# One wide fp32 product in place of eight transposes and eight narrow products in the merge stage of a test-time-memory attention and MoE kernel

## The chip, the cores and the metric

The kernel runs on one core of a Trainium2 chip, as one program. The metric is device time in microseconds (us) of the whole program. Three runs of the kernel before the change gave 2380.78, 2381.34 and 2384.04 us; their median is 2381.34 us. The engines are named PE (TensorE), DVE (VectorE), ACT (ScalarE), POOL (GpSimd) and SP (SyncE, which here only issues DMAs). PEld is the weight load of a PE instruction.

## What is computed

Two layers follow each other over x of 8 x 1024 tokens with 256 features: a sliding-window attention with a memory MLP that takes one gradient step (its output is merged with the attention's by two sigmoid gates), and a top-2 mixture of eight experts with a capacity of 640 tokens each. The part that the change touches is the seam between them:

```python
g1 = jax.nn.sigmoid(out_swa @ lin1.T)
g2 = jax.nn.sigmoid(out_mem @ lin2.T)
out_merged = g1 * out_swa + g2 * out_mem
...
x = x + attention_layer(layernorm(x), ...)        # x1, the residual sum
...
h = layernorm(x)                                   # input of the experts
logits = h @ gate_w.T + gate_b                     # 8 columns per token
probs = softmax(logits); topk_prob, topk_idx = top_k(probs, 2)
# the position of each token in its expert's queue is a running count over all tokens
x = x + experts(h, topk_idx, topk_prob)
```

Since the layer norm is (x1 - mean) * rstd, the kernel takes the logits from x1 itself: it multiplies x1 with the gate weights less their mean over the features ("centred gate"), which removes the mean's share, and scales by rstd afterwards.

## The kernel before

Four phases run one after the other: attention, gradient, merge and experts. Products of fp32 accuracy are made of three products of rounded halves (fp32r, `matmul_split`, L105: low x high, high x low, high x high). The change lies in `merge_phase`, which takes the 8192 tokens in 16 chunks (C = 0 to 15) of four blocks of 128 tokens. In it everything of a chunk lies transposed, features on partitions (`ga` is 128 x 2 x 512: two halves of 128 features, 512 tokens), while layer norm, router and output want tokens on partitions.

Each engine has its own list of work, written out by hand; semaphores (`signal`, `wait_ge`) tie the lists together, and a wait holds up everything behind it on its engine. Of one chunk C the PE list has, in this order:

- `hidden(C, 0..7)`: eight tiles of the memory MLP's hidden layer, six products of 512 columns each; behind the second of them `gate2(C-1)`, two tiles of the second gate of the chunk before;
- `residual(C-1, 0)`: eight transposes (L2019) of the merged sum `ga` of chunk C-1 into the PSUM tile `ps_r`, which wait for the sum (`merged`, DVE L2275);
- `router(C-1, 0)`: eight fp32 products (L2038) of the same blocks of `ga` with the centred gate, 8 columns each, two for each block of tokens, which add up in PSUM (`ps_l`, in the tile `ps_s`);
- `gate1(C)`: twelve products;
- `dispatch(C-2)` (from C = 2 on): five bf16 products (L2049, L2051) of the one-hot choices of chunk C-2, which count tokens per expert into `ps_c`, in the tile `ps_s` too; they wait for the one-hots (`chosen`, DVE L2394);
- `memory_out(C, ...)`: the output layer of the MLP, 48 products. In C = 15 a second `dispatch(14)` stands before its last quarter.

The DVE list of a chunk has, in this order: the multiplications of the hidden tiles (L2244), the gates of chunk C-1 and its merged sum (L2275), `weigh(C-2)` (L2372 to L2377), `choose_experts(C-2)` (L2384 to L2394), the rest of hidden tile 7 (`rest_hidden`, L2249), then `norm_stats(C-1)` (L2321 to L2330), DVE's `dispatch(C-2)`, `router(C-1)` (L2353, which scales the logits), `shift`, `norm_apply` and the rests for the next chunk. ACT makes the sigmoids (L2098), rounds the hidden tiles (L2103) and copies the transposed sum from PSUM to SBUF (`copy_x1`, L2159), from where it is stored and normed. POOL makes the rests of hidden tiles 0 to 6 (L2504).

The last chunk's sum (C = 15) is handled behind the loop in two parts.

Of the kernel before, what the change touches and what calls it, by code (L numbers as in the profile page):

```python
# [12 lines left out]
AX = mybir.AxisListType  # L13
# [1798 lines left out]
        sems.give_back(made)  # L1812


def merge_banks():

    out = []
    for C in range(NCH):
        out += [("gate2", C - 1, m) for m in range(KC) if C]
        out += [("gate1", C, m) for m in range(KC)] + [("om", C, m) for m in range(KC)]  # L1820
    return out + [("gate2", NCH - 1, m) for m in range(KC)]


def merge_phase(nc, io, sems, shared, routed, halves, g1, g2, b1n, b2n, chunk_in, first_w1, first_w2):
    with ExitStack() as ctx:
        made = []

        def sb(name, shape, dt=F32):
            return ctx.enter_context(nc.sbuf_tensor(name, shape, dt))
# [30 lines left out]
        x1 = [sb("x1_0", [P, GRP, D]), shared.oT[:].rearrange("p (j d) -> p j d", j=GRP)]  # L1860
        rows = routed.rows
        x2 = sb("xn2_full", [P, GRP, D])
        gate_c, ones_f = sb("gate_centred", [P, KC, E]), sb("m_ones_f", [P, P])
        stats, mv, rstd = sb("m_stats", [P, GRP, 6]), sb("m_mv", [P, GRP, 2]), sb("m_rstd", [P, 2, GRP])
        lg, below, pr = sb("logits", [P, GRP, E]), sb("logits_below", [P, GRP, E + TOPK]), sb("router_probs", [P, GRP, E + TOPK])
        sm = sb("router_sum", [P, 2, GRP])
# [10 lines left out]

        ps_z = [ps(f"m_ps_z{i}", [P, T]) for i in range(NZ)]
        ps_o = [ps(f"m_ps_o{i}", [P, T]) for i in range(2)]
        ps_r = ps("m_ps_r", [P, GRP, D])  # L1880
        ps_s = ps("m_ps_s", [P, 512])
        ps_l, ps_c = ps_s[:, 0:GRP * E], ps_s[:, GRP * E:]
        x1_v = io["out"].rearrange("(b p) d -> p b d", p=P)

        use = merge_banks()
# [14 lines left out]

        z_done = signal("m_z_done", hidden_of)
        gate1_done, gate2_done, om_done = (signal(f"m_{k}_done", kinds[k]) for k in ("gate1", "gate2", "om"))
        merged_T, logits_done = (signal(n, tails) for n in ("merged_T", "logits_done"))
        gate_summed = signal("gate_summed", [0])
        counts_done = signal("counts_done", chunks)

# [52 lines left out]
        def tensor(e):  # L1959
# [52 lines left out]
            def residual(C, n):  # L2012
# [6 lines left out]
                        i = e.transpose(ps_r[:, j, m * P:(m + 1) * P], ga[:, m, j * P:(j + 1) * P], ident[:])  # L2019
                i.then_inc(*merged_T(C, n))  # L2020

            def sum_gate():
                pe.wait_ge(*gate_in.at(0))
                pe.wait_ge(*const_set.at(4))
                for k in range(KC):
                    i = e.matmul(ps_l[:, 0:E], ones_f[:], gate[:, k], start=k == 0, stop=k == KC - 1)
                i.then_inc(*gate_summed(0))
# [13 lines left out]
            def dispatch(C):  # L2041
                pe.wait_ge(*chosen.at(C, 2))
                pe.wait_ge(*earlier_made.at(0))
                pe.wait_ge(*const_set.at(5))
                pe.wait_ge(*lg_scaled.at(C))
                n = SIZES[C]
                out = ps_c[:, 0:(n + 1) * n_hot].rearrange("p (j x) -> p j x", x=n_hot)
                ones_of = hot[:].rearrange("p j k x -> p j (k x)")
                e.matmul(out, earlier[:], ones_of[:, 0:n + 1], start=True, stop=False)  # L2049
                for i in range(n):  # L2050
                    x = e.matmul(out[:, i + 1:], ones[:], ones_of[:, i:i + 1].broadcast_to([P, n - i, n_hot]), start=False, stop=i == n - 1)  # L2051
                x.then_inc(*counts_done(C))

            for C in chunks:
                tail, sent = C >= 1, C >= 2
                hidden(C, 0)
                hidden(C, 1)
                if tail:
                    gate2(C - 1)
                for t in range(2, HC):  # L2060
                    hidden(C, t)
                if tail:
                    residual(C - 1, 0)
                    router(C - 1, 0)
                gate1(C)
                if C == 0:
                    sum_gate()
                if sent:
                    dispatch(C - 2)
                memory_out(C, 0, 0)  # L2070
                memory_out(C, 0, 1)
                memory_out(C, 1, 0)
                if C == NCH - 1:
                    dispatch(NCH - 2)
                memory_out(C, 1, 1)
# [16 lines left out]
        def scalar(e):  # L2092
# [58 lines left out]
            def copy_x1(C, n):  # L2151
# [4 lines left out]
                    act.wait_ge(*x2_made.at(*final_part(C - 2)))  # L2156
                else:
                    act.wait_ge(*x2_made.at(C, n))
                e.activation(x1[s][:, blocks], ps_r[:, blocks], ACTF.Copy).then_inc(*x1_made(C, n))  # L2159

            def split_x2(C, n):
                blocks = parts_of(C)[n]
# [73 lines left out]
        def vector(e):  # L2236
# [95 lines left out]
            def norm_apply(C, n):  # L2332
# [9 lines left out]
                dve.wait_ge(*const_set.at(3))  # L2342
                e.tensor_copy(routed.tails(C)[:, blocks, 0], tokens[:, C * GRP + blocks.start:C * GRP + blocks.stop]).then_inc(*numbered(C, n))

            def router(C):
                n, wide = SIZES[C], [P, SIZES[C], E]
                src = ps_l.rearrange("p (j x) -> p j x", x=E)
                dve.wait_ge(*logits_done.at(*final_part(C)))
                dve.wait_ge(*gate_b_in.at(0))
                dve.wait_ge(*chosen.at(C - 1, 0))  # L2350
                dve.wait_ge(*shifted.at(C - 1, 0))
                dve.wait_ge(*rstd_made.at(*final_part(C)))
                e.tensor_tensor(lg[:, 0:n], src[:, 0:n], rstd[:, 1, 0:n].unsqueeze(2).broadcast_to(wide), ALU.mult).then_inc(*lg_scaled(C))  # L2353
                dve.wait_ge(*lg_scaled.at(C))
# [72 lines left out]
            for C in chunks:  # L2427
# [26 lines left out]
                if C == 0:  # L2454
# [2 lines left out]
                    e.tensor_copy(earlier[:], before_f[:]).then_inc(*earlier_made(0))  # L2457
                    centre_gate()
                if tail:
                    norm_stats(C - 1, 0)  # L2460
                if sent:
                    dispatch(C - 2)
# [76 lines left out]
        def sync(e):  # L2539
# [15 lines left out]
            load_oT(0)  # L2555
            load_x(0)
            e.dma_start(gate[:], io["gateT"].rearrange("(c p) n -> p c n", p=P)).then_inc(*gate_in(0))
            e.dma_start(gate_b[:], io["gate_b"]).then_inc(*gate_b_in(0))
            e.dma_start(ident[:], io["ident"]).then_inc(*ident_in(0))
            e.dma_start(before_f[:], io["before"]).then_inc(*before_in(0))  # L2560
# [494 lines left out]
```

## Time and profile before

| | |
|---|---|
| median of three runs | 2381.34 us |
| the profiled execution's own time | 2381.39 us |
| its span, as the profile shows it | 2379.6 us |
| PE busy | 2335.8 us (98%) |
| DVE busy | 1691.1 us (71%) |
| ACT busy | 1608.7 us (68%) |
| POOL busy | 1394.9 us (59%) |
| the merge loop, chunks 0 to 15 | about 1392 to 1878 us of the span |

The profile is of one execution. The busy time of an engine is the time in which at least one of its instructions ran; matmuls overlap each other in it, so that the distance from start to start of neighbouring matmuls, and not the length of one, tells what one costs. "Idle before" is time in which an engine stood still ahead of an instruction, with what released it; such a releaser is inferred from semaphore events, and "issue" means that the profile shows none.

### The profile page before, as it was taken

Reading aid. Unit: us, or ns where it says so; the run is one execution under the profiler, and the core shown is the slowest. Engines: PE = TensorE matmul, PEld = TensorE weight load, DVE = VectorE, ACT = ScalarE, POOL = GpSimd, SP = SyncE. Lnnn points to the kernel's source line nnn. Section 1 sums busy time; section 2 is a strip of 40 time slices with the busy share of each in tenths; the row PEclk is TensorE's granted clock in tenths of the full one; section 3 lists DMA queues with packets and bytes.
Section 4 is the critical chain, followed back from the end, with each engine's and each line's share of the span. In section 5 each row is a group of like instructions: output and inputs, shape, how many; then the busy total and the mean of one; then the engine's idle time right before and its main releaser. Section 6 shows DMA issues by size and latency. Waiting matters only on the chain. (4 is left out here: it accounts for less than half of the span.)

```text
span 2379.6 us, 40041 instructions
## 1 busy us (share of the span) xinstructions
PE 2335.8 (98%) x14851; PEld 2080.9 (87%) x14851; DVE 1691.1 (71%) x3668; ACT 1608.7 (68%) x2459; POOL 1394.9 (59%) x1000
## 2 busy tenths in 40 slices
PE   7999999999999999999999999999999899999998
PEld 6888888788888888888888978888888789999998
DVE  7777776666666666666666677777777667777776
ACT  5887888757777777777777647777777545554453
POOL 3665566567766766666677735666666543343433
PEclk9999999999999999999999999999999999999999
DMA  4222221542332223222333222333222055555551
GB/s 132 85 84 72 94 76 54 215 126 65 72 69 63 63 64 66 63 62 65 69 68 68 80 92 89 107 103 101 96 91 72 22 156 140 141 151 144 145 141 58
DMA packets 295394, 221.74 MB, mean 93 GB/s; under 512 B 189282, under 2 KB 262023, under 8 KB 295072
## 3 DMA queue, kind: packets, MB, share of 16 engines
q1 hardware_dynamic: 281376, 188.74, 29.1%
q0 software_dynamic: 13824, 30.44, 4.2%
q8 instruction: 118, 1.93, 0.3%
q14 instruction: 76, 0.62, 0.1%
HBM read 113.30 MB, written 72.12 MB: 78 GB/s over the span
## 5 line engine op out<-in xcount | busy, mean ns | idle before, releaser
L2780 ACT ACTIVATE e_hf<-e_ps_z,e_b 128x640 f32<-128x640 f32 x128 | 102.0, 797 | 213.2 <-PE e_ps_z L105 181.3
L2504 POOL TENSOR_TENSOR m_hl<-m_hf,m_hh 128x512 fp32r<-128x512 f32 x112 | 159.6, 1447 | 100.8 <-ACT m_hh L2103 98.5
L2908 POOL DMA_INDIRECT out<-e_ys,slot_token x80 | 83.4, 1042 | 216.3 <-DVE e_ys L2859 210.8
L105 PE MATMUL e_ps_y<-r_w_h,e_hl 128*128 128x256 f32 x640 | 180.3, 282 | 0.1
L105 PE MATMUL e_ps_y<-r_w_l,e_hh 128*128 128x256 f32 x640 | 178.9, 279 | 0.0
L105 PE MATMUL e_ps_y<-r_w_h,e_hh 128*128 128x256 f32 x640 | 178.6, 279 | 0.0
L1686 POOL TENSOR_TENSOR halves_l<-hT_full,halves_h 128x512 fp32r<-128x512 f32 x120 | 153.7, 1303 | 38.2 <-ACT halves_h L1337 38.2
L932 POOL DMA_INDIRECT xbuf_d<-xn,scatter_rows x128 | 139.0, 1086 | 62.3 <-issue 35.6
L789 POOL TENSOR_TENSOR prob<-prob,softmax_small 128x1024 f32<-128x1024 f32 x65 | 123.2, 1896 | 71.1 <-DVE softmax_small L705 71.1
L105 PE MATMUL e_ps_z<-slotsT_h,w_l 128*128 128x320 f32 x512 | 158.9, 310 | 0.7 <-issue 0.7
L105 PE MATMUL e_ps_z<-slotsT_h,w_h 128*128 128x320 f32 x512 | 158.9, 310 | 0.0
L105 PE MATMUL e_ps_z<-slotsT_l,w_h 128*128 128x320 f32 x512 | 158.9, 310 | 0.0
L2244 DVE SCALAR_TENSOR_TENSOR m_hf<-m_ps_z,new_b,m_sig 128x512 f32<-128x512 f32 x128 | 95.9, 749 | 86.1 <-ACT m_sig L2098 63.3
L1544 DVE TENSOR_TENSOR new_w2T<-g_bank,new_w2T 128x512 f32<-128x512 f32 x128 | 88.6, 692 | 92.5 <-PE g_bank L105 92.5
L1331 ACT ACTIVATE hT_full<-h_wordsT 128x2048 uint16<-128x2048 uint16 x60 | 153.2, 2553 | 0.0
L105 PE MATMUL g_bank<-dpred_h,h_l 128*128 128x256 f32 x520 | 147.4, 283 | 1.7 <-DVE shared_x L1537 1.7
L105 PE MATMUL g_bank<-halves_h,keys_l 128*128 128x256 f32 (+1 forms) x528 | 147.4, 279 | 1.1 <-DVE halves_l L1495 1.1
L1551 DVE TENSOR_TENSOR new_w1T<-g_bank,new_w1T 128x512 f32<-128x512 f32 x128 | 88.5, 692 | 83.6 <-PE g_bank L105 83.6
L105 PE MATMUL g_bank<-halves_l,keys_h 128*128 128x256 f32 (+1 forms) x528 | 147.8, 280 | 0.0
L105 PE MATMUL g_bank<-halves_h,keys_h 128*128 128x256 f32 (+1 forms) x528 | 147.3, 279 | 0.0
L105 PE MATMUL g_bank<-dpred_l,h_h 128*128 128x256 f32 x520 | 147.1, 283 | 0.0
L105 PE MATMUL g_bank<-dpred_h,h_h 128*128 128x256 f32 x520 | 147.1, 283 | 0.0
(371 smaller groups left out, 8967.4 us busy)
## 6 DMA issues: line engine op xcount, KB each, us to landing
shared_xT<-xT_d SPq DMA_DIRECT2D x64, 256.0 KB, 3.6
new_w1T<-in_W SPq DMA_DIRECT2D x16, 1024.0 KB
new_w2T<-in_W SPq DMA_DIRECT2D x16, 1024.0 KB
xbuf_d<-new_w1T SPq DMA_DIRECT2D x16, 650.0 KB, 8.4
shared_x<-in_x SPq DMA_DIRECT2D x16, 512.0 KB, 4.1
xn_d<-xn SPq DMA_DIRECT2D x32, 256.0 KB, 2.5
xT_d<-shared_xT SPq DMA_DIRECT2D x32, 256.0 KB, 2.7
oT_d<-shared_oT SPq DMA_DIRECT2D x32, 256.0 KB, 2.6
```

Of the source, the lines that this page charges most:

```text
L105: i = e.matmul(out, a, b, start=first and not onto and n == 0, stop=last and n == len(terms) - 1, skip_group_check=onto)
L789: e.tensor_tensor(p[:], p[:], sm[:, 3].unsqueeze(2).broadcast_to([P, HEADS, 2 * P]), ALU.mult).then_inc(*prob_made(g))
L932: e.indirect_dma_start(io["xbuf_d"][k], bass.IndirectOffsetOnAxis(ap=self.slot[C % 2][:, k, j:j + 1], axis=0), self.rows[C % 3][:, j], Non ...
L1331: e.activation(hT_f[b][:].bitcast(U16).rearrange("p (n s) -> p s n", s=2), wordsT[b][:].rearrange("p (s k) t -> p s (k t)", s=2), ACTF.Cop ...
L1544: e.tensor_tensor(dst, bank("g2", p, t)[:], dst, ALU.add).then_inc(*g2_added(p, t))
L1551: e.tensor_tensor(dst, bank("g1", p, t)[:], dst, ALU.add).then_inc(*g1_added(p, t))
L1686: e.tensor_tensor(hTl[:, ks, block[b]], hT_f[b][:, hc].rearrange("p (k t) -> p k t", k=4), hTh[:, ks, block[b]], ALU.subtract).then_inc(*m ...
L2244: e.scalar_tensor_tensor(hf[r][:, 0:N], ps_z[r][:, 0:N], b1n[:, t:t + 1], sig[r][:, 0:N], ALU.add, ALU.mult).then_inc(*h_made(C, t))
L2504: e.tensor_tensor(hl[:, t, 0:N], hf[(HC * C + t) % NZ][:, 0:N], hh[:, t, 0:N], ALU.subtract).then_inc(*h_low(C, t))
L2780: e.activation(hf[(HC * i + t) % NHF][:].rearrange("p (s n) -> p s n", s=2), ps_z[t % 2][:, :, 0:HALF], ACTF.Relu, bias=b1[:, i % E, t:t + ...
L2908: e.indirect_dma_start(io["out"], bass.IndirectOffsetOnAxis(ap=token[i % 2][:, b:b + 1], axis=0), ys[:, b], None, bounds_check=NT - 1, oob ...
```

## The change

For chunks 0 to 14, `residual` and `router` on PE become one function, `residual_router(C)`. A block of 128 features x 128 tokens of `ga` is loaded as weights once and multiplied, in fp32, with 136 columns: the identity (128) and the centred gate of that half of the features (8). The first 128 columns of the result are the transposed block; the last 8 are this half's share of the logits. The two halves go to different places in PSUM, since the identity columns must not add up; so the shares are summed afterwards, by a new DVE instruction (`sum_logits`), which reads 128 x 4 x 8 x 2 values from PSUM and writes 128 x 32 to `lg` in SBUF. It stands ahead of `norm_stats(C-1)` in the DVE list. L2353 reads `lg` instead of PSUM.

The tiles `ps_r` (two banks) and `ps_s` (one) become one tile `ps_t` of three banks: eight units of 171 columns, three to a bank, so that no product crosses a bank; behind them `ps_l` and `ps_c`. The third bank then holds the units 6 and 7 and the counts of `dispatch`. So PE's `dispatch(C-2)`, in iteration C, gets two waits more: for ACT's copy of the units of chunk C-1 (`x1_made`) and for DVE's sum (`lg_summed`) of chunk C-1. The second dispatch of iteration 15 waits for the same two as its first. The right operand `turned` (identity and gate side by side) gets its identity by two more DMAs of 64 KB, which SP issues at the start of the merge phase ahead of six others. Chunk 15 keeps the old functions, on the new tile.

```diff
--- before.py
+++ after.py
@@ -1812,6 +1812,9 @@
         sems.give_back(made)
 
 
+UNIT = 171
+
+
 def merge_banks():
 
     out = []
@@ -1860,7 +1863,8 @@
         x1 = [sb("x1_0", [P, GRP, D]), shared.oT[:].rearrange("p (j d) -> p j d", j=GRP)]
         rows = routed.rows
         x2 = sb("xn2_full", [P, GRP, D])
-        gate_c, ones_f = sb("gate_centred", [P, KC, E]), sb("m_ones_f", [P, P])
+        turned = sb("ident_and_gate", [P, KC, P + E])
+        gate_c, ones_f = turned[:, :, P:], sb("m_ones_f", [P, P])
         stats, mv, rstd = sb("m_stats", [P, GRP, 6]), sb("m_mv", [P, GRP, 2]), sb("m_rstd", [P, 2, GRP])
         lg, below, pr = sb("logits", [P, GRP, E]), sb("logits_below", [P, GRP, E + TOPK]), sb("router_probs", [P, GRP, E + TOPK])
         sm = sb("router_sum", [P, 2, GRP])
@@ -1877,9 +1881,10 @@
 
         ps_z = [ps(f"m_ps_z{i}", [P, T]) for i in range(NZ)]
         ps_o = [ps(f"m_ps_o{i}", [P, T]) for i in range(2)]
-        ps_r = ps("m_ps_r", [P, GRP, D])
-        ps_s = ps("m_ps_s", [P, 512])
-        ps_l, ps_c = ps_s[:, 0:GRP * E], ps_s[:, GRP * E:]
+        ps_t = ps("m_ps_t", [P, 3 * 512])
+        units = ps_t[:, 0:GRP * KC * UNIT].rearrange("p (j k x) -> p j k x", k=KC, x=UNIT)
+        ps_r = ps_t[:, 0:GRP * D].rearrange("p (j d) -> p j d", j=GRP)
+        ps_l, ps_c = ps_t[:, GRP * KC * UNIT:GRP * KC * UNIT + GRP * E], ps_t[:, GRP * KC * UNIT + GRP * E:]
         x1_v = io["out"].rearrange("(b p) d -> p b d", p=P)
 
         use = merge_banks()
@@ -1900,7 +1905,10 @@
 
         z_done = signal("m_z_done", hidden_of)
         gate1_done, gate2_done, om_done = (signal(f"m_{k}_done", kinds[k]) for k in ("gate1", "gate2", "om"))
-        merged_T, logits_done = (signal(n, tails) for n in ("merged_T", "logits_done"))
+        merged_T = signal("merged_T", tails)
+        logits_done = signal("logits_done", [u for u in tails if u[0] == NCH - 1])
+        turned_in = signal("m_turned_in", range(KC), 16)
+        lg_summed = signal("m_lg_summed", chunks[:-1])
         gate_summed = signal("gate_summed", [0])
         counts_done = signal("counts_done", chunks)
 
@@ -2019,6 +2027,21 @@
                         i = e.transpose(ps_r[:, j, m * P:(m + 1) * P], ga[:, m, j * P:(j + 1) * P], ident[:])
                 i.then_inc(*merged_T(C, n))
 
+            def residual_router(C):
+                pe.wait_ge(*merged.at(C, 0))
+                for k in range(KC):
+                    pe.wait_ge(*turned_in.at(k))
+                pe.wait_ge(*gate_centred.at(0))
+                pe.wait_ge(*x1_made.at(*final_part(C - 1)))
+                if C:
+                    pe.wait_ge(*lg_summed.at(C - 1))
+                if C >= 2:
+                    pe.wait_ge(*placed.at(C - 2, 1))
+                for j in range(SIZES[C]):
+                    for k in range(KC):
+                        i = e.matmul(units[:, j, k, 0:P + E], ga[:, k, j * P:(j + 1) * P], turned[:, k], start=True, stop=True)
+                i.then_inc(*merged_T(C, 0))
+
             def sum_gate():
                 pe.wait_ge(*gate_in.at(0))
                 pe.wait_ge(*const_set.at(4))
@@ -2042,7 +2065,12 @@
                 pe.wait_ge(*chosen.at(C, 2))
                 pe.wait_ge(*earlier_made.at(0))
                 pe.wait_ge(*const_set.at(5))
-                pe.wait_ge(*lg_scaled.at(C))
+                if C < NCH - 1:
+                    read = min(C + 1, NCH - 2)
+                    pe.wait_ge(*x1_made.at(read, 0))
+                    pe.wait_ge(*lg_summed.at(read))
+                else:
+                    pe.wait_ge(*lg_scaled.at(C))
                 n = SIZES[C]
                 out = ps_c[:, 0:(n + 1) * n_hot].rearrange("p (j x) -> p j x", x=n_hot)
                 ones_of = hot[:].rearrange("p j k x -> p j (k x)")
@@ -2060,8 +2088,7 @@
                 for t in range(2, HC):
                     hidden(C, t)
                 if tail:
-                    residual(C - 1, 0)
-                    router(C - 1, 0)
+                    residual_router(C - 1)
                 gate1(C)
                 if C == 0:
                     sum_gate()
@@ -2156,7 +2183,11 @@
                     act.wait_ge(*x2_made.at(*final_part(C - 2)))
                 else:
                     act.wait_ge(*x2_made.at(C, n))
-                e.activation(x1[s][:, blocks], ps_r[:, blocks], ACTF.Copy).then_inc(*x1_made(C, n))
+                if C < NCH - 1:
+                    e.activation(x1[s][:].rearrange("p j (k d) -> p (j k) d", k=KC),
+                                 units[:, :, :, 0:P].rearrange("p j k d -> p (j k) d"), ACTF.Copy).then_inc(*x1_made(C, n))
+                else:
+                    e.activation(x1[s][:, blocks], ps_r[:, blocks], ACTF.Copy).then_inc(*x1_made(C, n))
 
             def split_x2(C, n):
                 blocks = parts_of(C)[n]
@@ -2342,13 +2373,24 @@
                 dve.wait_ge(*const_set.at(3))
                 e.tensor_copy(routed.tails(C)[:, blocks, 0], tokens[:, C * GRP + blocks.start:C * GRP + blocks.stop]).then_inc(*numbered(C, n))
 
+            def sum_logits(C):
+                dve.wait_ge(*merged_T.at(C, 0))
+                dve.wait_ge(*x1_made.at(C, 0))
+                dve.wait_ge(*chosen.at(C - 1, 0))
+                dve.wait_ge(*shifted.at(C - 1, 0))
+                e.tensor_reduce(lg[:], units[:, :, :, P:P + E].rearrange("p j k x -> p j x k"), AX.X, ALU.add).then_inc(*lg_summed(C))
+
             def router(C):
                 n, wide = SIZES[C], [P, SIZES[C], E]
                 src = ps_l.rearrange("p (j x) -> p j x", x=E)
-                dve.wait_ge(*logits_done.at(*final_part(C)))
                 dve.wait_ge(*gate_b_in.at(0))
-                dve.wait_ge(*chosen.at(C - 1, 0))
-                dve.wait_ge(*shifted.at(C - 1, 0))
+                if C < NCH - 1:
+                    src = lg[:]
+                    dve.wait_ge(*lg_summed.at(C))
+                else:
+                    dve.wait_ge(*logits_done.at(*final_part(C)))
+                    dve.wait_ge(*chosen.at(C - 1, 0))
+                    dve.wait_ge(*shifted.at(C - 1, 0))
                 dve.wait_ge(*rstd_made.at(*final_part(C)))
                 e.tensor_tensor(lg[:, 0:n], src[:, 0:n], rstd[:, 1, 0:n].unsqueeze(2).broadcast_to(wide), ALU.mult).then_inc(*lg_scaled(C))
                 dve.wait_ge(*lg_scaled.at(C))
@@ -2457,6 +2499,7 @@
                     e.tensor_copy(earlier[:], before_f[:]).then_inc(*earlier_made(0))
                     centre_gate()
                 if tail:
+                    sum_logits(C - 1)
                     norm_stats(C - 1, 0)
                 if sent:
                     dispatch(C - 2)
@@ -2555,6 +2598,8 @@
             load_oT(0)
             load_x(0)
             e.dma_start(gate[:], io["gateT"].rearrange("(c p) n -> p c n", p=P)).then_inc(*gate_in(0))
+            for k in range(KC):
+                e.dma_start(turned[:, k, 0:P], io["ident"]).then_inc(*turned_in(k))
             e.dma_start(gate_b[:], io["gate_b"]).then_inc(*gate_b_in(0))
             e.dma_start(ident[:], io["ident"]).then_inc(*ident_in(0))
             e.dma_start(before_f[:], io["before"]).then_inc(*before_in(0))
```

In the list of PE, at `residual` and `router` of one chunk, `m_ps_r` and `m_ps_s` are the old PSUM tiles, `m_ps_t` is the new one, `r_ident` the identity, `gate` is `ga`:

```order
-L2019 MATMUL m_ps_r<-r_ident,gate 128x128 x8
-L2038 MATMUL m_ps_s<-gate_centred,gate 128x8 x8
+L2042 MATMUL m_ps_t<-ident_and_gate,gate 128x136 x8
 L105 MATMUL m_ps_o<-halves_h,keys_l 128x512
 L105 MATMUL m_ps_o<-halves_l,keys_h 128x512
```

Sixteen rows' worth of instructions became eight; the twelve products of `gate1` behind them stayed.

PE's `dispatch` in the middle of the loop, before the change, with the semaphores it waits for in brackets (semaphores are used again from phase to phase, so their names tell nothing of what they mean here; the one of this row is the one-hots'):

```order
L105 MATMUL m_ps_o<-halves_h,keys_h 128x512
L2049 MATMUL m_ps_s<-router_hot,m_before 128x80 [waits exp_made_51]
L2051 MATMUL m_ps_s<-router_hot,m_ones 128x64
L2051 MATMUL m_ps_s<-router_hot,m_ones 128x48
```

The same place after the change, where `h_low_v_68` is the copy's signal, `score_done_29` that of the sum of the logits, and `av_full_53` that of the one-hots:

```order
L105 MATMUL m_ps_o<-halves_h,keys_h 128x512
L2077 MATMUL m_ps_t<-router_hot,m_before 128x80 [waits score_done_29,h_low_v_68,av_full_53]
L2079 MATMUL m_ps_t<-router_hot,m_ones 128x64
L2079 MATMUL m_ps_t<-router_hot,m_ones 128x48
```

The place of the instruction is the same; two waits came in.

The list of DVE at the end of the hidden tiles, before the change, from the one-hots to the norm:

```order
L2394 TENSOR_TENSOR router_hot<-expert_ids,router_idf 128x4x8
L2249 TENSOR_TENSOR m_hl<-m_hf,m_hh 128x512 [waits out_full_56]
L2321 BN_STATS m_stats<-x_0 128x6 [waits sig_half_66]
L2321 BN_STATS m_stats<-x_0 128x6 x3
```

And after it:

```order
L2436 TENSOR_TENSOR router_hot<-expert_ids,router_idf 128x4x8
L2280 TENSOR_TENSOR m_hl<-m_hf,m_hh 128x512 [waits w2T_high_58]
L2381 TENSOR_REDUCE logits<-m_ps_t 128x32 [waits pt_high_52,h_low_v_68,qk_done_26]
L2352 BN_STATS m_stats<-x_0 128x6 x4
```

The new TENSOR_REDUCE stands behind the rest of hidden tile 7, and all of DVE's later work of the chunk behind it.

## Rows read from the trace of the kernel before

**Rows 1.** The page's first part: busy time, share, instructions of each engine.
```profile
PE 2335.8 (98%) x14851; PEld 2080.9 (87%) x14851; DVE 1691.1 (71%) x3668; ACT 1608.7 (68%) x2459; POOL 1394.9 (59%) x1000
```
**Rows 2.** Busy time by stretch: three of the merge loop, and two with stalls.
```profile
core 0: us, PE busy (x) PEld busy (x) DVE busy (x) ACT busy (x) POOL busy (x), PEclk, DMA share, GB/s
1433.00:1466.00 33.00, 33.00 (x169) 27.76 (x169) 22.40 (x45) 23.78 (x36) 13.45 (x11) 1.00 0.25 74
1466.00:1496.00 30.00, 30.00 (x146) 24.57 (x145) 22.88 (x63) 21.31 (x32) 19.28 (x16) 1.00 0.30 100
...
1408.00:1414.00 6.00, 4.97 (x22) 3.75 (x21) 4.57 (x7) 2.12 (x5) 2.00 (x1) 1.00 0.65 205
1877.00:1900.00 23.00, 15.07 (x81) 12.52 (x80) 14.47 (x67) 9.29 (x12) 8.97 (x10) 0.87 0.02 3
```
**Rows 3.** Timeline of PE in iteration 3 (start us, us, engine, line, instruction, count).
```profile
1493.83 0.40 PE L105 MATMUL m_ps_z<-halves_h,w_h 128*128 128x512 f32 x1
1494.06 1.03 PE L2019 MATMUL m_ps_r<-r_ident,gate 128*128 128x128 f32 x8
1494.93 1.85 PE L2038 MATMUL m_ps_s<-gate_centred,gate 128*128 128x8 f32 x16
1496.64 0.47 PE L105 MATMUL m_ps_o<-halves_h,keys_l 128*128 128x512 f32 x1
```
**Rows 4.** Timeline of all engines around dispatch in iteration 3.
```profile
1497.68 1.01 ACT L2159 ACTIVATE x<-m_ps_r 128x1024 f32<-128x1024 f32 x1
...
1499.03 0.69 DVE L2249 TENSOR_TENSOR m_hl<-m_hf,m_hh 128x512 fp32r<-128x512 f32 x1
...
1499.48 0.21 PE L2049 MATMUL m_ps_s<-router_hot,m_before 128*128 128x80 bf16 x1
...
1499.63 1.40 DVE L2321 BATCH_NORM_STATS2 m_stats<-x 128x6 f32<-128x256 f32 x4
```
**Rows 5.** The same pair in iterations 2 and 15, the first and last of fourteen.
```profile
1468.40 0.69 DVE L2249 TENSOR_TENSOR m_hl<-m_hf,m_hh 128x512 fp32r<-128x512 f32 x1
1468.86 0.21 PE L2049 MATMUL m_ps_s<-router_hot,m_before 128*128 128x80 bf16 x1
...
1866.64 0.69 DVE L2249 TENSOR_TENSOR m_hl<-m_hf,m_hh 128x512 fp32r<-128x512 f32 x1
...
1867.11 0.21 PE L2049 MATMUL m_ps_s<-router_hot,m_before 128*128 128x80 bf16 x1
```
**Rows 6.** Timeline at the start of iteration 3; in brackets the idle time before.
```profile
1487.39 0.69 ACT L2098 ACTIVATE m_sig<-m_ps_z,new_b 128x512 f32<-128x512 f32 x1 [2.95 <-PE m_ps_z L105]
...
1488.11 0.75 DVE L2244 SCALAR_TENSOR_TENSOR m_hf<-m_ps_z,new_b,m_sig 128x512 f32<-128x512 f32 x1 [3.41 <-ACT m_sig L2098]
...
1490.23 8.52 POOL L2504 TENSOR_TENSOR m_hl<-m_hf,m_hh 128x512 fp32r<-128x512 f32 x6 [4.25 <-ACT m_hh L2103]
```
**Rows 7.** The two TENSOR_REDUCE of DVE (ns min/median/max, first and last start).
```profile
L2412 DVE TENSOR_REDUCE router_pos<-router_pos_e x16: 220/221/222, 1471.6 to 1898.7; 128x8 f32<-128x64 f32 x16
...
L2372 DVE TENSOR_REDUCE router_sum<-router_probs x16: 169/171/178, 1463.8 to 1897.6; 128x4 f32<-128x32 f32 x16
```
**Rows 8.** Timeline of the last dispatch, which waits for the one-hots.
```profile
1896.22 0.29 DVE L2394 TENSOR_TENSOR router_hot<-expert_ids,router_idf 128x32 bf16<-128x32 f32 x2
...
1896.57 0.21 PE L2049 MATMUL m_ps_s<-router_hot,m_before 128*128 128x80 bf16 x1 [1.90 <-DVE router_hot L2394]
```
**Rows 9.** Timeline of PE in the experts: products of 256 columns.
```profile
1999.84 0.28 PE L105 MATMUL e_ps_y<-r_w_l,e_hh 128*128 128x256 f32 x1
...
2003.96 0.28 PE L105 MATMUL e_ps_y<-r_w_h,e_hl 128*128 128x256 f32 x1
```
**Rows 10.** Timeline of PE in iteration 1, which has no dispatch.
```profile
1433.05 1.03 PE L2019 MATMUL m_ps_r<-r_ident,gate 128*128 128x128 f32 x8
1433.92 1.85 PE L2038 MATMUL m_ps_s<-gate_centred,gate 128*128 128x8 f32 x16
1435.62 0.47 PE L105 MATMUL m_ps_o<-halves_h,keys_l 128*128 128x512 f32 x1
```
**Rows 11.** Start of the merge phase: SP's queue, ACT's first use, PE's wait.
```profile
1396.52 0.43 SPq L2564 DMA_DIRECT2D lin_f<-in_lin1T  x1
...
1400.17 0.64 ACT L2145 ACTIVATE keys_h<-lin_f 128x512 fp32r<-128x512 f32 x1
...
1410.81 0.47 PE L105 MATMUL m_ps_o<-m_hh,r_w_l 128*128 128x512 f32 x1 [1.03 <-DVE m_hl L2249]
```
**Rows 12.** DMA issues of that stretch: KB each, median us to landing.
```profile
lin_f<-in_lin1T SPq DMA_DIRECT2D x1, 256.0 KB, 3.6
```

## Prediction

> **What bounds the kernel now.** I read the busy times first [rows 1]: PE is busy in 98% of the span, no other engine in more than 71%. Then busy time by stretch over the merge loop [rows 2]: from 1433 to 1496 us PE is busy in 33.00 of 33.00 and 30.00 of 30.00 us at a granted clock of 1.00, DVE in about three quarters. So in the loop every us that PE is given or spared counts fully, and every wait that reaches PE costs fully.
>
> The timeline of PE in iteration 3 tells what the two old functions cost [rows 3]: the transposes start at 1494.06, the narrow products at 1494.93, the first product of `gate1` at 1496.64. Together 2.58 us: 0.87 for 8 transposes (0.109 each) and 1.71 for 8 fp32 products, which the trace shows as 16 passes (0.107 each). Iteration 1 gives 2.57 [rows 10].
>
> Then I looked at what stands where the new waits come in. `dispatch` starts at 1499.48; ACT's copy of the sum has ended at 1498.69, but DVE is still at the rest of hidden tile 7 (1499.03 to 1499.72), and only then comes the place where the new sum of the logits is put [rows 4]. The same in the first and last of the fourteen such iterations: L2249 ends at 1469.09 against 1468.86, and at 1867.33 against 1867.11 [rows 5]. DVE thus reaches the new instruction about 0.22 us after PE has begun `dispatch` today.
>
> Last, what sets DVE's time there. At the start of the iteration ACT stood idle for 2.95 us until PE had made a tile, DVE 3.41 us for ACT, POOL 4.25 us for ACT [rows 6]. All three are tied to PE's start of the iteration, and until `copy_x1` nothing in their lists needs what PE does behind the hidden tiles. DVE's arrival stays where it is, counted from the start of the iteration, however fast PE gets through the transposes.
>
> **The change part by part.**
>
> *PE, 24 passes become 16.* An fp32 product shows as two passes, so the new function has 16 passes of 136 columns. No row has a wide fp32 product. From below: a narrow pass takes 0.107 us, which for 8 columns must be the load of the weights, and that load stays; 16 x 0.107 = 1.71 us. From above: if each of the two passes streamed the columns twice, each time at the transpose's 0.109 us per 128, a product would cost 4 x 0.109 x 136/128 = 0.463, eight of them 3.71 us. The nearest row to the value I take: a transpose of 128 fp32 columns takes 0.109 us in one pass, about as long as 256 columns of fp32r, 36 of which start from 1999.84 to 2003.96, so every 0.118 us [rows 9]. So I take two steps a column and pass: 0.118 x 272/256 = 0.125 us, 16 passes 2.0 us. PE would be spared 2.58 - 2.0 = 0.58 us an iteration, 15 times.
>
> On this the Trainium skill speaks against the change. The transpose goes with 0.109 us for 128 columns [rows 3]; "TensorE: Matmul & The Clock Gate" (section Terms) says that the transpose mode is four times faster for fp32 than the ordinary mode. By that rule the eight products would take 3.71 us instead of 2.0. No run of the kernel before has a wide ordinary product to test it.
>
> *The new wait of `dispatch`.* In an iteration from 2 to 15 DVE must first do the sum of the logits. Today the instruction behind L2249 starts at 1499.63, 0.09 us ahead of L2249's end [rows 4]. The sum reads 64 values a partition. A TENSOR_REDUCE over 64 takes 0.221 us, over 32 it takes 0.171 [rows 7]; the new one has 32 outputs where that has 8, and reads PSUM. Bounds: 0.17 from below, 0.35 (1.40 us for four BN_STATS of 256 values, rows 4, each) from above; I take 0.23. From DVE's end to PE's start the last dispatch, the one that waits for DVE today, shows 1896.51 to 1896.57, 0.06 us [rows 8]. So `dispatch` starts 0.22 - 0.09 + 0.23 + 0.06 = 0.42 us later, counted from the iteration's start, than today. PE arrives 0.58 us earlier than today and stands for 1.00 us: the whole of the saving is lost in the wait, and 0.42 us more. Behind the waiting instruction stand the four other count products and the 48 of `memory_out`, and so the next iteration. 14 x 0.42 = 5.9 us.
>
> ACT's copy needs the end of the products, at 1494.06 + 2.0 + 0.2, about 1496.3; it starts at 1497.68 in ACT's own order [rows 4]. Nothing there.
>
> *Iteration 1* has no `dispatch`: -0.6 us.
>
> *DVE behind the sum* does all its work of the iteration 0.23 us later, PE 0.42 us later, so PE meets no new wait there. L2353 from SBUF instead of PSUM: nothing. PE's idle of 1.00 us an iteration should not lower the clock: a wait of 1.03 us at 1410.81 left it at 1.00 in that stretch [rows 2, 11]; the stretch 1877 to 1900, in which PE is busy only 15.07 of 23.00 us, has 0.87 [rows 2].
>
> *Two more DMAs* on SP's queue ahead of `lin1`: each issue takes 0.43 us and 0.48 to the next, so `lin1` is issued at 1397.5 instead of 1396.52 [rows 11] and, 3.6 us later [rows 12], lands at 1401.1; ACT wants it at 1400.17 [rows 11]. ACT stands up to 0.9 us there, once. PE waits for DVE's rest of tile 7 at 1410.81 anyway, which comes at the end of POOL's chain; between 0 and 0.9 us, I take 0.1.
>
> *The sum:* 5.9 - 0.6 + 0.1 = +5.4 us on the profiled execution's own 2381.39 us (span 2379.6 us), so 2386.8 us. That execution lies 0.05 us from the median of the three runs, 2381.34, so the same figure holds against it: +0.23%.
>
> **The rivals.**
>
> *A. The wait is hidden, faster.* If `lg_summed` came before PE reaches `dispatch`, the loop would keep the saving: 15 x 0.58 = 8.7 us, 2372.8 us. It is decided by DVE's arrival: it would have to be a full 1.00 us earlier. For it speaks that DVE has idle time (a quarter of the loop, rows 2), part of which may be a wait for things that come earlier with PE. Against it: this idle time lies at the iteration's start, where PE itself is awaited [rows 6], and fourteen iterations show the same 0.22 us within 0.02.
>
> *B. The wide fp32 pass is twice as long as I take it.* 3.71 us for the function: PE reaches `dispatch` 3.71 - 2.58 = 1.13 us later than today, behind DVE's sum, so that the wait is gone and 15 x 1.13 = 17 us are paid: 2398.4 us. For it speaks that no row shows a wide product, and that the narrow ones, bound by their weights, cannot tell how their columns stream; against it that a product shows two passes, not four, and that one transpose pass of 128 columns already takes as long as 256 of fp32r [rows 3, 9]. The Trainium skill's rule above would give this case. The point from which the pass's length counts at all is (2.58 + 0.42)/16 = 0.19 us; below that PE waits for DVE in any case.
>
> *C. More is late.* DVE's list, 0.23 us longer, or ACT's exponent behind it, makes PE wait once more in an iteration, or the reduction takes the 0.35 us of its upper bound: 14 x 0.12 = 1.7 us for the latter, up to 0.4 us an iteration, 6 us, for both: to about 2392.
>
> *D. Nothing that can be told.* The forecast's own sum with a reduction of 0.17 us and no DMA stall is +4.5 us, inside 0.2%.
>
> **How the numbers follow.** No change here means within 0.2%, 4.8 us, about what a measurement of this kernel can tell: 2376.6 to 2386.1. The forecast (D being its lower part) gets 0.78, A 0.07, B 0.10, C 0.05. The forecast's own range is 2384 to 2390: the reduction's bounds give -0.8 and +1.7 us, the DMAs up to +0.8, the hand-over between DVE and PE (0.06 us, from one row) perhaps 0.05 more or less, 0.7 us. Of its 0.78, 0.56 lies above 2386.1 and 0.22 below. Slower: 0.56 + 0.10 + 0.05 = 0.71; same: 0.22; faster: 0.07. The range 2382.5 to 2394 takes in the forecast and C and leaves out A and B, 0.17.
>
> **What would show it.** In the profile after: L2042 with 16 records an iteration, the next product of `gate1` 2.0 us behind the first of them (3.7 by rival B); the new TENSOR_REDUCE behind the rest of tile 7, 0.2 to 0.3 us long; ahead of PE's L2077 an idle time of 0.8 to 1.1 us in fourteen iterations, released by that TENSOR_REDUCE; the distance from one dispatch to the next 31.05 us instead of the 30.63 that the thirteen steps from 1468.86 to 1867.11 give [rows 5]; the clock at 1.00 in the loop. The forecast is wrong if PE does not wait at L2077 (A or B, by the length of L2042), or if the distance is the same and the time lies elsewhere.

## The result

| | before | after |
|---|---|---|
| median, 8 runs each | 2380.79 us (2380.18 to 2384.04) | 2387.39 us (2386.51 to 2389.22) |
| ratio to before, 95% interval | | 1.0025 (1.0016 to 1.0034) |
| span of the profiled execution | 2379.6 us | 2385.2 us |

The change makes the kernel 0.25% slower: 6.6 us by the medians, 5.6 by the two spans.

The page after, first part (busy us, share of the span, instructions):

```profile
PE 2327.2 (98%) x14731; PEld 2069.1 (87%) x14731; DVE 1693.8 (71%) x3683; ACT 1607.8 (67%) x2459; POOL 1391.0 (58%) x1000
```

PE has 120 records fewer than in [rows 1] and 8.6 us less to do, and yet the kernel is slower: PE stands still more.

Busy time by stretch after (us, then busy time and instructions of each engine, granted clock, DMA share, GB/s):

```profile
1466.00:1496.00 30.00, 28.83 (x133) 23.25 (x132) 22.30 (x62) 21.08 (x31) 19.09 (x16) 1.00 0.32 104
```

Where PE was busy for all of 30.00 us [rows 2], it now stands 1.17 us. The clock is still at its full level, 1.00.

The waits of PE in the merge loop after (who waited for whom, us in total, times, longest):

```profile
PE m_ps_t L2077 <- DVE logits L2381: 16.3, 14, 1.2
...
PE m_ps_o L105 <- ACT gate L2136: 0.5, 1, 0.5
```

Fourteen waits of `dispatch` for the new sum, 1.16 us each. The second line, one wait in iteration 1, looks small; it turns out to be the more interesting one below.

The timeline of PE in iteration 3 after, to be laid beside [rows 3]:

```profile
1495.05 0.40 PE L105 MATMUL m_ps_z<-halves_h,w_h 128*128 128x512 f32 x1
1495.28 2.02 PE L2042 MATMUL m_ps_t<-ident_and_gate,gate 128*128 128x136 f32 x16
...
1497.02 0.28 PE L2042 MATMUL m_ps_t<-ident_and_gate,gate 128*128 128x136 f32 x1
1497.05 0.48 PE L105 MATMUL m_ps_o<-halves_h,keys_l 128*128 128x512 f32 x1
```

The second line is the whole group; the third is its last pass by itself. The wide products are 16 passes, as the narrow ones were, and take 1.77 us from the start of the first to the start of the next instruction: 0.111 us a pass on average, 0.81 us less than the 2.58 of before. From start to start inside the group it is 0.116 us (15 distances from 1495.28 to 1497.02); only the last pass is followed after 0.03 us. The length of the group's row, 2.02 us, also contains the last pass up to its end.

The timeline around `dispatch` in iteration 3 after, to be laid beside [rows 4] (in brackets the idle time before it):

```profile
1500.27 0.69 DVE L2280 TENSOR_TENSOR m_hl<-m_hf,m_hh 128x512 fp32r<-128x512 f32 x1
...
1500.87 0.22 DVE L2381 TENSOR_REDUCE logits<-m_ps_t 128x32 f32<-128x64 f32 x1
...
1501.23 0.20 PE L2077 MATMUL m_ps_t<-router_hot,m_before 128*128 128x80 bf16 x1 [1.17 <-DVE logits L2381]
...
1501.47 0.47 PE L105 MATMUL m_ps_o<-m_hh,r_w_l 128*128 128x512 f32 x1
```

The line of before that [rows 4] leaves out, the first product of `memory_out`:

```profile
1499.63 0.48 PE L105 MATMUL m_ps_o<-m_hh,r_w_l 128*128 128x512 f32 x1
```

Counted from the first instruction on `ga` in PE's list (1494.06 before, 1495.28 after), DVE's rest of tile 7 ends at 5.66 before and 5.68 after: DVE did not move. `dispatch` went from 5.42 to 5.95, and `memory_out` behind it from 5.57 to 6.19.

The first and the last of the fourteen, for [rows 5]:

```profile
1470.02 0.20 PE L2077 MATMUL m_ps_t<-router_hot,m_before 128*128 128x80 bf16 x1 [1.17 <-DVE logits L2381]
...
1876.08 0.20 PE L2077 MATMUL m_ps_t<-router_hot,m_before 128*128 128x80 bf16 x1 [1.17 <-DVE logits L2381]
```

406.06 us for thirteen steps, 31.24 each, against 398.25 and 30.63 before: 0.60 us an iteration.

### The profile page after: what moved, and what is told of

The parts are those of the page before. It is cut to its first block and busy times, and to the rows that moved or that the text cites. A ratio compares the mean times of both kernels' runs of the same rounds, so it can differ in the third digit from the quotient of the medians.

```text
span 2385.2 us, 39833 instructions
## 1 busy us (share of the span) xinstructions
PE 2327.2 (98%) x14731; PEld 2069.1 (87%) x14731; DVE 1693.8 (71%) x3683; ACT 1607.8 (67%) x2459; POOL 1391.0 (58%) x1000
```

## The experiments

They ran on three other chips than the first comparison (e1 to e4 on one, e5 to e8 on another, e9 and e10 on a third); there the kernel before has medians of 2376.45, 2376.51 and 2376.64 us instead of 2380.8. So each is compared with the runs of the kernel before on its own chip; the times expected for e1 to e4 start from the first chip's 2387.4 us and are to be read 4.3 us lower. And beside the time I give the mean distance from one `dispatch` to the next in the loop ("step"), which one profile tells to 0.05 us and in which nothing outside the loop takes part.

| run | median us | ratio (95% interval) | step us |
|---|---|---|---|
| e8 before again | 2376.18 | 0.9997 (0.9988 to 1.0006) | 30.64 |
| e5 after again | 2381.19 | 1.0023 (1.0013 to 1.0032) | 31.23 |
| e1 split | 2380.42 | 1.0021 (1.0012 to 1.0030) | 31.20 |
| e2 sum twice | 2383.85 | 1.0035 (1.0022 to 1.0049) | 31.36 |
| e3 sum early | 2374.49 | 0.9992 (0.9983 to 1.0001) | 30.63 |
| e4 late | 2373.76 | 0.9990 (0.9981 to 0.9999) | 30.55 |
| e9 gate only | 2379.78 | 1.0016 (1.0007 to 1.0025) | 31.23 |
| e6 late, gate | 2362.80 | 0.9944 (0.9930 to 0.9958) | 29.85 |
| e7 the same moves on before | 2377.56 | 1.0006 (0.9997 to 1.0015) | 30.65 |
| e10 late, gate, split | 2376.06 | 1.0000 (0.9991 to 1.0009) | 30.66 |

**The two kernels again (e5, e8).**

> The changed kernel once more, unedited, to have it on the same chip as the experiments, whose kernel before ran at 2376.45 us. Theory: 31.24 us from dispatch to dispatch as in its first profile, +0.25% against before, 2382.5 us. Rival: another chip also changes the loop.

> The kernel before, unedited, for its profile on this chip. Theory: 30.63 us from dispatch to dispatch as on the other chip; its lower total time (2376.45 against 2380.8 us) lies outside the loop. Rival: the loop is faster too.

The loop is the same on both chips, 31.23 and 30.64 us a step. The difference between the chips lies behind the loop, at one place: the first product that PE makes of the last chunk's rounded output. Before the change on the first chip, and on the second (e8):

```profile
1884.41 0.58 PE L105 MATMUL m_ps_z<-keys_h,keys_l 128*128 128x256 f32 x1 [5.46 <-DVE keys_l L2283]
```

```profile
1880.91 0.39 PE L105 MATMUL m_ps_z<-keys_h,keys_l 128*128 128x256 f32 x1 [1.56 <-DVE keys_l L2283]
```

PE waits for DVE there, and DVE for ACT, which rounds the same output. In the two profiles of the first chip ACT starts this rounding (at 1882.88 before) 3.9 and 3.5 us after PE's last product has ended, in the ten others 0.03 to 0.04 us after it. From the second `dispatch` of iteration 15 to the last `dispatch` the kernel before takes 20.82 us on the first chip and 15.69 in e8, the kernel after 21.57 and 15.68 (e5). That is 5.1 and 5.9 us, where the spans of the two chips differ by 4.8 and 6.1. What held ACT is not shown: the profile names a DMA, `silu_rest<-in_w2T`, which belongs to an earlier phase. It falls on both kernels and cancels in their comparison, but for 0.75 us.

**e1: the products taken apart, the wait kept.**

```diff
                 for j in range(SIZES[C]):
                     for k in range(KC):
-                        i = e.matmul(units[:, j, k, 0:P + E], ga[:, k, j * P:(j + 1) * P], turned[:, k], start=True, stop=True)
+                        e.transpose(units[:, j, k, 0:P], ga[:, k, j * P:(j + 1) * P], turned[:, k, 0:P])
+                for j in range(SIZES[C]):
+                    for k in range(KC):
+                        i = e.matmul(units[:, j, k, P:P + E], ga[:, k, j * P:(j + 1) * P], turned[:, k, P:], start=True, stop=True)
```

> The changed kernel, with the wide products of residual_router taken apart again into eight transposes and eight narrow products; the new waits, the sum on VectorE and the PSUM layout stay. Theory (VectorE's sum sets when dispatch starts, PE's passes before it are covered): 24 passes, 2.6 us instead of 2.0, the wait ahead of dispatch shrinks from about 1.17 to about 0.6 us, dispatch to dispatch stays at 31.24 us, time as the changed kernel's, 2387.4 us within 1. Rival (PE's work counts, the wide products are worth their 0.56 us): 15 x 0.56 = 8.4 us more, 2395.8 us, 31.8 us from dispatch to dispatch.

Measured: 31.20 us a step and 2380.42 us; PE has 24 passes again, 2.58 us of work. The wait in iteration 3, from the timeline:

```profile
1500.92 0.20 PE L2080 MATMUL m_ps_t<-router_hot,m_before 128*128 128x80 bf16 x1 [0.33 <-DVE logits L2384]
```

0.33 us instead of 1.17: what PE works more it waits less. The slowdown does not depend on the wide products at all; what is left for it is the new sum, its wait or the new layout in PSUM, and e3 decides between these. The time is 0.8 us below e5's, where the rival wanted 8.4 us more: it is out.

**e2: the sum twice.**

```diff
+                e.tensor_reduce(lg_again[:], units[:, :, :, P:P + E].rearrange("p j k x -> p j x k"), AX.X, ALU.add)
                 e.tensor_reduce(lg[:], units[:, :, :, P:P + E].rearrange("p j k x -> p j x k"), AX.X, ALU.add).then_inc(*lg_summed(C))
```

> The changed kernel, with the sum of the logits issued twice, the first time into a tile that nobody reads, 0.22 us each. Theory (VectorE's arrival counts fully): dispatch starts 0.22 us later in 14 iterations, 31.46 us from one to the next, +3.1 us, 2390.5 us. Rival (the added time comes from the wide products or the PSUM layout, and VectorE has slack): no change, 2387.4 us.

Measured: 31.36 us a step, 0.12 more, not 0.22, and 2383.85 us, 2.7 more than e5. The direction is the theory's, the size in the loop is half of it. The timeline in iteration 3 shows why:

```profile
1500.62 0.21 DVE L2382 TENSOR_REDUCE logits_again<-m_ps_t 128x32 f32<-128x64 f32 x1
...
1500.75 0.21 DVE L2383 TENSOR_REDUCE logits<-m_ps_t 128x32 f32<-128x64 f32 x1
```

The second starts 0.13 us behind the first, though each lasts 0.21: here an instruction that waits for nothing starts before its predecessor's end, and what it adds to the queue is the distance of starts.

**e3: the sum one instruction earlier.**

```diff
+                if tail:
+                    sum_logits(C - 1)
                 rest_hidden(C, 7)
...
                 if tail:
-                    sum_logits(C - 1)
                     norm_stats(C - 1, 0)
```

> The changed kernel, with the sum of the logits one instruction earlier in VectorE's list, ahead of the rest of hidden tile 7 (0.69 us) instead of behind it. Theory: the sum ends 0.6 us earlier, behind the one-hots, dispatch starts 0.6 us earlier in 14 iterations, 30.63 us from one to the next, 14 x 0.6 = 8.5 us less: 2379 us, about as the kernel before; PE still waits about 0.5 us at dispatch. Rival (the loss lies elsewhere): 2387.4 us.

Measured: 30.63 us a step, 0.60 less, as expected, the wait at `dispatch` 0.56 us:

```profile
1500.17 0.20 PE L2077 MATMUL m_ps_t<-router_hot,m_before 128*128 128x80 bf16 x1 [0.56 <-DVE logits L2381]
```

The time, 2374.49 us, is 0.9992 of before, with an interval that just reaches 1: this one move of DVE's instruction, with the sum, its wait and the new layout all left in, takes back the whole loss. All that the change costs in the loop is thus DVE's lateness.

**e4: `dispatch` later on PE.**

```diff
-                if sent:
-                    dispatch(C - 2)
                 memory_out(C, 0, 0)
+                if sent:
+                    dispatch(C - 2)
```

> The changed kernel, with dispatch one quarter of memory_out (12 products, 2.8 us) later in PE's list, so that VectorE's sum is long made. Theory as the trace of iteration 1 suggests it (the next thing that PE needs is the PSUM bank that ACT's sigmoid of gate1 frees, and this comes behind ACT's copy of the sum, so that only 0.13 us of 0.56 can be kept): PE waits about 0.45 us ahead of memory_out, 30.50 us from dispatch to dispatch, 2379 us. Rival (only the wait of dispatch eats the saving, as rival A of the prediction had it): 30.07 us, 2372.5 us.

This run tests what iteration 1 of the changed kernel had shown. It has no `dispatch`, so by my prediction it should have kept the saving. It kept 0.14 us of it: from the first instruction on `ga` to `memory_out` it has 5.27 us (1433.76 to 1439.03) instead of 5.41 (1433.05 to 1438.46). The timeline of that iteration, before and then after:

```profile
1437.57 0.59 ACT L2109 ACTIVATE gate<-m_ps_o 128x512 f32<-128x512 f32 x1
...
1438.46 0.40 PE L105 MATMUL m_ps_o<-m_hh,r_w_l 128*128 128x512 f32 x1
```

```profile
1437.39 1.01 ACT L2187 ACTIVATE x<-m_ps_t 128x1024 f32<-128x1024 f32 x1
...
1438.30 1.08 ACT L2136 ACTIVATE gate<-m_ps_o 128x512 f32<-128x512 f32 x2
1439.03 0.47 PE L105 MATMUL m_ps_o<-m_hh,r_w_l 128*128 128x512 f32 x1 [0.48 <-ACT gate L2136]
```

`memory_out(C, 0, 0)` writes the PSUM bank that `gate1(C, 0)` used. ACT's sigmoid must read it first, and stands in ACT's list behind the copy of the sum (1.01 us). Before the change the bank came free about 0.3 us before PE wanted it (the first sigmoid of iteration 1 ended at 1438.16, the product started at 1438.46), so that no engine stood for it. Measured in e4: 30.55 us a step where 30.50 was expected, and 2373.76 us; and now the wait stands there in every iteration (15 times, 7.0 us in total), as iteration 4 shows:

```profile
1529.57 0.47 PE L105 MATMUL m_ps_o<-m_hh,r_w_l 128*128 128x512 f32 x1 [0.46 <-ACT gate L2136]
```

With the wait for DVE gone, most of the saving still does not arrive. The price of the prediction's rival A, worked out as if `dispatch` were the only obstacle, is refuted by this run.

**e9: the bank freed early, `dispatch` left.**

```diff
-                    copy_x1(C - 1, 0)
                     gate1(C, 0)
+                    copy_x1(C - 1, 0)
```

> The changed kernel with the second of the two moves alone: the first sigmoid of gate1 ahead of the copy of the sum on ScalarE, dispatch left where it is. Theory (the two waits stand one behind the other, and this frees only the second): PE still waits 1.17 us at dispatch for VectorE's sum, 31.23 us from dispatch to dispatch, time as the changed kernel's on this chip, 2381.2 us within 1. Rival (the bank alone was what cost the time): 29.9 us and about 2363 us as with both moves.

Measured: 31.23 us a step and 1.16 us of wait at `dispatch`, as in the changed kernel; the wait in iteration 1 is gone. The time came out 1.4 us below e5's instead of within 1, on another chip; their intervals against before overlap, and half a us of it is iteration 1's.

**e6: both moves.** The edit of e4 and that of e9 together.

> The changed kernel, with dispatch one quarter of memory_out later on PE (as in the run before) and, on ScalarE, the first sigmoid of gate1 ahead of the copy of the sum instead of behind it, so that the PSUM bank that memory_out wants is free earlier. Theory (two waits stand one behind the other, VectorE's sum and then this bank; with both gone the 0.56 us of the wide products come through): PE waits at neither, 30.07 us from dispatch to dispatch, 15 x 0.56 = 8.4 us less than before: 0.9965 of it, 2368 us. Rival (a third wait, from the scatters on GpSimd or from the copy that is now late, takes its place): 30.3 to 30.6 us, 2371 to 2376 us.

Measured: 2362.80 us, 0.9944 of before, 13.7 us less; 29.85 us a step. PE is busy throughout the loop again:

```profile
1466.00:1496.00 30.00, 30.00 (x143) 24.59 (x142) 23.42 (x68) 21.98 (x34) 20.61 (x17) 1.00 0.33 107
```

The theory's direction holds, no third wait took over in the loop. The expected 2368 us were 5 us too high: I had still used 0.56 us for the saving, where 0.81 stands in the profile after (30.64 - 0.81 = 29.83), and had left out what the changed kernel saves behind the loop (below). This is the version that beats both kernels.

**e7 and e10: the same moves without the wide products.** e7 puts both moves on the kernel before; e10 takes e6 and splits the products as in e1.

> The kernel before, without the wide products, with the same two moves: dispatch one quarter of memory_out later on PE, the first sigmoid of gate1 ahead of the copy on ScalarE. Theory (before the change PE waits at neither place, so the moves alone bring nothing): 30.63 us from dispatch to dispatch, ratio 1.000. Rival (the moves bring time by themselves, and the wide products little): below 0.999.

> The changed kernel with both moves and the wide products taken apart again into eight transposes and eight narrow products (same layout, sum and waits). Theory (with no wait left, PE's passes count fully, 2.58 us against 1.77): 29.81 + 0.81 = 30.62 us from dispatch to dispatch, 15 x 0.81 = 12.2 us more than with the wide products, 2375 us. Rival (the gain of the run with both moves came from the moves or the layout): below 2369 us.

Measured: e7 1.0006, 30.65 us a step; e10 1.0000, 30.66 us. The moves alone bring nothing, on either layout; 30.66 - 29.85 = 0.81 us an iteration is what the wide products are worth once nothing waits, and the two medians, 2376.06 and 2362.80, lie 13.3 us apart, where 15 x 0.81 = 12.2 were expected.

## Why the prediction was right, and where it was not

The forecast, 2386.8 us and slower by 0.23%, came within 0.6 us of the median, and its mechanism is confirmed: PE waits at `dispatch` in fourteen iterations for the new sum, DVE's arrival is tied to the start of the iteration (e1, e3), and the saving on PE disappears in the wait. But that the sum came so close is luck: the wait was put 2.5 us too low, the gain of iteration 1 half a us too high, and some 4 us that the changed kernel's profiles give back behind the loop stood in no term.

- *The passes.* Predicted 0.125 us, 2.0 us for sixteen; measured 1.77 us. The distance of 0.116 us inside the group is what the transpose's 0.109 us for 128 columns gives for 136 (0.109 x 136/128 = 0.116), so a length in proportion to the columns was the right picture, but the 256-column row was the wrong price for it; and the last pass is followed after 0.03 us. In the same stretch a transpose takes 0.109 us and a wide product two passes, 0.22 to 0.23 us: a factor of two. By the rule of the Trainium skill ("TensorE: Matmul & The Clock Gate", Terms), that the transpose mode is four times faster for fp32, and with the transpose's 0.109 us taken as the time of its columns, eight products would take 3.71 us; the trace disagrees with this sum, and the measurement decides. Whether the rule fails here or only the use of the 0.109 us no run shows: a narrow pass of 8 columns takes as long, 0.107 us, so the transposes too may be held by the load of their weights and not by their columns. Rival B is out.
- *The wait.* Predicted 0.42 us later in each of fourteen iterations, measured 0.60. This term of the sum was mis-sized, by 2.5 us in all. Sized right: where DVE's sum starts (0.09 us ahead of the end of L2280), its length (0.22 for 0.23). Sized wrong: from its end, 1501.09, to PE's start at 1501.23 it is 0.14 us and not the 0.06 of the one row I had [rows 8]; and from `dispatch` to `memory_out` it is 0.24 us out of this wait, against 0.15 in the running stream of before. Not every wait costs this: behind the last `dispatch`, for which PE had stood 1.90 us [rows 8], the first product after the counts starts after 0.15 us (1896.57 to 1896.72, the line below), and its 0.06 us come back in the profile after (1906.33 to 1906.39). All waits for the new sum in e1, e2, e3 and e9 have 0.14 to 0.15 and 0.23 to 0.24. What makes the difference no run tests. The term is 14 x 0.60 = 8.4 us, not 5.9.

```profile
1896.72 0.48 PE L2079 MATMUL m_ps_z<-keys_h 128*128 128x512 f32 x1
```

- *Iteration 1.* Predicted -0.6 us, measured -0.14: the step that failed. I had looked for what the new wait delays, and not for what is late next when PE comes early. Behind `dispatch` stands the bank that ACT frees, 0.3 us ahead of PE's demand before the change. That also spoils rival A's price of 8.7 us (2381.4 - 8.7 is 2372.7, not 2372.8 us): without DVE's wait about 15 x 0.14, 2 us, could have been had (e4 has 0.09 us a step).
- *The DMAs.* `lin1` was awaited, but shortly. The timelines of SP and ACT after, for [rows 11]:

```profile
1398.17 0.43 SPq L2609 DMA_DIRECT2D lin_f<-in_lin1T  x1
...
1401.13 0.63 ACT L2172 ACTIVATE keys_h<-lin_f 128x512 fp32r<-128x512 f32 x1 [0.24 <-DMA lin_f<-in_lin1T]
...
1411.51 0.47 PE L105 MATMUL m_ps_o<-m_hh,r_w_l 128*128 128x512 f32 x1 [0.90 <-DVE m_hl L2280]
```

  ACT stood 0.24 us; the phase began 0.70 us later in this execution (PE's first product at 1392.52 instead of 1391.82), and PE's product at 1411.51 is 0.70 later too. So the DMAs cost PE nothing (I took 0.1).
- *Behind the loop.* Not in the prediction. From the first `dispatch` to the last one in the loop the profiles differ by +7.8 us in both pairs (before and after; e8 and e5), yet the spans by 5.6 and 4.3. Behind the last `dispatch` of all it is 483.0 us to the end before and 478.8 after, and 483.0 against 478.9 in e8 and e5. A good part of it goes with the granted clock. Two stretches of the kernel before, from the last `dispatch` to the end of the phase and on to the first output product of the experts:

```profile
1896.57:1909.81 13.24, 12.94 (x54) 10.26 (x54) 4.02 (x19) 2.56 (x5) 4.17 (x4) 0.87 0.13 42
1909.81:1933.30 23.49, 20.45 (x119) 18.90 (x119) 15.67 (x25) 9.17 (x13) 16.33 (x14) 0.93 0.85 225
```

  and the same two after:

```profile
1906.39:1917.98 11.59, 11.29 (x54) 9.09 (x54) 4.02 (x19) 2.56 (x5) 4.16 (x4) 1.00 0.16 50
1917.98:1938.92 20.94, 19.21 (x118) 17.33 (x119) 15.60 (x25) 9.19 (x13) 15.66 (x14) 1.00 0.91 244
```

  They are 1.65 and 2.55 us shorter after, together all of the 4.2. The first stretch has the same instructions at the full clock (2.4 GHz; the mean of 0.87 mixes it with stretches at 1.2); over the twelve profiles of this study it takes either 11.6 or 13.2 us, in kernels of both kinds. Of the second, the part behind the experts' first product with loaded slots takes 14.2 us in six profiles, where the stretch's clock is 1.00, and 15.5 to 15.7 in six (the three with the old products and layout, and e4, e9, e10), where it is 0.92 or 0.93: 1.5 of the 2.55 us. The other 1.0 us lies ahead of that product: the three profiles with the old products and layout (before, e7, e8) need 7.8 to 8.1 us from the start of the experts to their first product with loaded slots, the nine with the new layout 6.4 to 7.2 us, e10 with its 24 passes among the latter. So some 1.3 us on average belong to the changed program and not to the loop; what makes them, I have not found.

The account of the first pair of spans: 0.7 for the later start of the phase, -0.14 in iteration 1, 8.4 in the fourteen others, 0.1 + 0.75 from the last `dispatch` in the loop to the last of all, and -4.2 behind it, makes +5.6. If what goes with the clock (3.2 of the 4.2) and the later start are taken as no part of the change, it is about +8, and the forecast's +5.4 some 3 us short. The medians, 6.6 us apart on the first chip and 5.0 (e5 against e8) on the second, contain such clocks in shares that the profiles of single executions don't tell.

## What to carry to other kernels

Work taken from the engine that bounds the kernel is worth nothing until the next thing it waits for comes earlier too; list, behind the place of the saving, every wait with its slack before the change (here DVE about -0.5 us once the sum is in its way, and ACT's bank +0.3 us), and move those along with it: the wide products alone cost 5 to 7 us, with two reordered lines they gained 13.7.

A new wait should be put where the awaited instruction has long been made: the same sum one place earlier on DVE, or `dispatch` twelve products later on PE, each took the loss away.

## What I had not expected of the hardware

- An ordinary fp32 product of 136 columns costs hardly more than one of 8, 4%: 0.111 us a pass against 0.107, two passes each. Here the 128 columns more were nearly free.
- The wait for the new sum costs PE 0.23 us beyond DVE's end: 0.14 us from the end of DVE's record to PE's start, and 0.09 more in the first products behind it. Behind the last `dispatch` of the kernel before, after 1.90 us of standing, it is 0.06 us and nothing more.
- Of two TENSOR_REDUCE of 0.21 us in a row the second starts 0.13 us behind the first.
